# Grams in bursts of eight units, four units to a PSUM bank, in a recommendation model's interaction and MLP

## The reference

```
dots  = einsum('bfd,bgd->bfg', bottom_output, bottom_output)   # (2048, 27, 27)
pairs = dots[:, TRIL_I, TRIL_J]                                # 351 of them
x     = concatenate([bottom_mlp_output, pairs, pad], axis=1)   # (2048, 480)
for w, b in ((w0, b0), (w1, b1), (w2, b2), (w3, b3)):          # 480-1024-1024-512-256
    x = relu(x @ w.T + b)
y = x @ w_out.T + b_out                                        # (2048, 1)
```

## Time and profile before

| | |
|---|---|
| median of three runs | 501.91 us |
| profiled execution, its own time | 498.37 us |
| its span | 496.2 us |
| TensorE busy (products) | 476.7 us, 96% |
| TensorE weight loads | 440.1 us, 89% |
| VectorE, ScalarE, GpSimd busy | 199.3, 186.0, 132.1 us |
| grams on TensorE (L641) | 4096 records, 47.9 us |
| copies of grams on ScalarE (L767) | 112, 373 ns each |
| granted clock of TensorE, mean | 0.986 |

### The profile page before, as it was taken

How to read it: one execution, slowest core, us unless ns; L and a number is a source line. 1 busy time by engine, 2 the same in 40 slices (tenths; PEclk the granted TensorE clock), 3 DMA queues, 4 the chain that set the end, 5 groups by cost and what they waited for, 6 DMA issues and landing times.

```text
span 496.2 us, 17883 instructions
## 1 busy us (share of the span) xinstructions
PE 476.7 (96%) x7119; PEld 440.1 (89%) x7119; DVE 199.3 (40%) x461; ACT 186.0 (37%) x457; POOL 132.1 (27%) x242
## 2 busy tenths in 40 slices
PE   6767999999999999999999999999999999999998
PEld 5666988998989998999999998999899998999897
DVE  1155635435542453245432543255423544143211
ACT  3345633425333353325342443235332533234222
POOL 1630321121322241222222231223222141224231
PEclk9789999999999999999999999999999999999999
DMA  8996976656666566754674656755665564300000
GB/s 209 264 325 152 272 108 109 107 108 122 99 99 126 95 112 99 123 111 79 101 111 102 109 88 97 127 107 88 103 104 117 92 96 69 76 29 0 1 1 0
DMA packets 281088, 53.83 MB, mean 108 GB/s; under 512 B 265126, under 2 KB 279230, under 8 KB 281022
## 3 DMA queue, kind: packets, MB, share of 16 engines
q1 hardware_dynamic: 279090, 52.22, 55.6%
q10 hardware_dynamic: 1932, 0.61, 0.5%
HBM read 45.71 MB, written 7.09 MB: 106 GB/s over the span
## 4 chain that ended last, share of the span: by engine, by line
PE 84%; SPq 7%; DMA 6%; issue 2%; DVE 1%; ACT 1%; ACTq 0%; DVEq 0%
PE acc L690 38%; PE acc L683 23%; PE acc L685 11%; PE gram_ps L641 7%; SPq L454 5%; DMA rows<-in_r_bottom_output_dram 2%; DMA pairs<-blocks 2%; PE gram_ps L609 2%; SPq L436 1%; DMA blocks<-grams 1%; DVE xt L886 1%; PE side_ps L614 1%; PE acc L614 0%; SPq L406 0%; SPq L401 0%
## 5 line engine op out<-in xcount | busy, mean ns | idle before, releaser
L554 POOL TENSOR_TENSOR h_a<-h_full,h_a 128x256 fp32r<-128x256 f32 x96 | 71.8, 751 | 173.7 <-DVE h_a L905 173.7
L690 PE MATMUL acc<-h_a,w_hi 128*128 128x256 f32 x592 | 116.4, 288 | 0.0
L683 PE MATMUL acc<-h_a,w_hi 128*128 128x512 f32 x280 | 100.0, 401 | 0.0
L690 PEld LDWEIGHTS acc<-h_a,w_hi 128*128 128x128 f32 x592 | 94.6, 191 | 1.9 <-issue 0.2
L554 POOL TENSOR_TENSOR h_b<-h_full,h_b 128x256 fp32r<-128x256 f32 x64 | 47.1, 736 | 170.1 <-DVE h_b L905 170.1
L776 ACT ACTIVATE h_full<-acc,small_t 128x256 f32<-128x256 f32 x98 | 46.3, 474 | 121.4 <-PE acc L690 120.5
L690 PE MATMUL acc<-h_a,w_lo 128*128 128x256 f32 x296 | 79.4, 283 | 0.1
L794 ACT ACTIVATE h_full<-acc,small_t 128x256 f32<-128x256 f32 x77 | 36.5, 474 | 113.8 <-PE acc L685 113.8
L685 PE MATMUL acc<-h_a,w_lo 128*128 128x256 f32 x280 | 78.6, 281 | 0.0
L886 DVE STREAM_TRANSPOSE xt<-rows 128x512 f32<-128x512 f32 x112 | 73.5, 689 | 10.4 <-DMA rows<-in_r_bottom_output_dram 10.3
L899 DVE TENSOR_TENSOR h_full<-acc,h_full 128x256 f32<-128x256 f32 x77 | 32.7, 424 | 111.7 <-ACT h_full L794 111.7
(11 more groups left out here) (69 smaller groups left out, 555.3 us busy)
## 6 DMA issues: line engine op xcount, KB each, us to landing
rows<-in_r_bottom_output_dram SPq DMA_DIRECT2D x444, 64.0 KB, 2.1
blocks<-grams SPq DMA_DIRECT2D x30, 216.0 KB, 4.0
w_raw<-in_L_rec_w_dram SPq DMA_DIRECT2D x6, 1024.0 KB, 7.9
early_rows<-in_r_bottom_output_dram SPq DMA_DIRECT2D x12, 224.0 KB, 5.9
stage_pairs<-in_L_rec_w_dram SPq DMA_DIRECT2D x1, 1408.0 KB, 10.6
w_raw<-in_L_rec_w_dram SPq DMA_DIRECT2D x2, 512.0 KB, 7.8
mlp_rows<-r_bottom_mlp_output_dram SPq DMA_DIRECT2D x8, 128.0 KB, 2.4
pairs<-blocks SPq DMA_DIRECT2D x8, 126.0 KB
```

The lines of the kernel that those rows point to most:

```text
L554: nc.gpsimd.tensor_tensor(h[:, m, 1, :], h_full[:, slot % FULL_RING, :], h[:, m, 0, :].bitcast(F32), ALU.subtract).then_inc(split_done, 1)
L683: nc.tensor.matmul(found, weight(w_hi, layer, m, k), src.rearrange("p h n -> p (h n)"), start=(k == 0), stop=False)
L690: last = nc.tensor.matmul(found[:, 0:CHUNK], weight(wp, layer, m, k), src[:, xp, :], start=(k == 0 and n == 0), stop=(ends and n == 2))
```

## The change

The grams of a chunk are made in two bursts of eight units, at the hooks after 108 and 252 products, where there were four bursts of four. For chunks 1 to 7 four units share a PSUM bank, each in its 128 columns, so that the 16 units fill four banks. ScalarE then copies a whole bank in one instruction (`move_bank`), two of them behind each other at each burst. `grams_done` counts one a bank for these chunks, and TensorE waits for it only at the first unit of a bank. Chunk 0's own units keep their banks and copies.

```
-HOOK, FIRST_HOOK, UNITS_A_HOOK, HOOKS_A_BURST = 36, 6, 2, 2
+HOOK, FIRST_HOOK, UNITS_A_HOOK, HOOKS_A_BURST = 36, 6, 2, 4
+UNITS_A_BANK = 4
+BANKS_USED = UNITS // UNITS_A_BANK
...
+        def gram_found(d, u):
+
+            if isinstance(d, int) and d == 0:
+                return first_gram_found(u)
+            first = u % UNITS_A_BANK * P
+            return gram_ps[:, u // UNITS_A_BANK, first:first + P].rearrange("p (j f) -> p j f", f=QUAD)[:, :, 0:FEATS]
+
+        def bank_found(q):
+
+            return gram_ps[:, q, :].rearrange("p (j f) -> p j f", f=QUAD)[:, :, 0:FEATS]
+
+        def bank_place(q):
+
+            n = UNITS_A_BANK * UNIT_GROUPS
+            return grams[:, :, q * n:(q + 1) * n].rearrange("p g j -> p j g")
+
+        def banks_count(d, q):
+
+            return UNITS + (d - 1) * BANKS_USED + q + 1
...
-                sp.wait_ge(grams_done, d * UNITS + UNITS)
+                sp.wait_ge(grams_done, UNITS + d * BANKS_USED)
...
-                if isinstance(d, int) and d == 1 and u < GRAM_RING:
+                if isinstance(d, int) and d == 0:
+                    if u >= GRAM_RING:
+
+                        pe.wait_ge(grams_done, u + 1 - GRAM_RING)
+                elif isinstance(d, int) and d == 1:
                     if u == 0:
 
                         pe.wait_ge(w_done, LATE_WEIGHTS)
-                elif not (isinstance(d, int) and d == 0 and u < GRAM_RING):
-
-                    pe.wait_ge(grams_done, d * UNITS + u + 1 - GRAM_RING)
+                elif u % UNITS_A_BANK == 0:
+
+                    pe.wait_ge(grams_done, banks_count(d - 1, u // UNITS_A_BANK))
...
-            def move_gram(d, u):
-
-                act.wait_ge(gram_done, d * UNITS + u + 1)
-                if u == 0:
+            def move_bank(d, q):
+
+                act.wait_ge(gram_done, d * UNITS + (q + 1) * UNITS_A_BANK)
+                if q == 0:
 
                     act.wait_ge(spilled, d * GROUP * 16)
-                nc.scalar.activation(gram_place(u), gram_found(u), ACT.Copy).then_inc(grams_done, 1)
+                nc.scalar.activation(bank_place(q), bank_found(q), ACT.Copy).then_inc(grams_done, 1)
...
-                        move_gram(c + step[1], step[2])
+                        if step[2] % UNITS_A_BANK == UNITS_A_BANK - 1:
+                            move_bank(c + step[1], step[2] // UNITS_A_BANK)
```

More of the change, by code:

```diff
@@ L385, in samples, with first_gram_found, first_gram_place @@
             return xt[:, u % XT_RING].rearrange("p j (s f) -> p j s f", s=GROUP)[:, :, :, 0:FEATS]
-        def gram_found(u):
+        def first_gram_found(u):
             return gram_ps[:, u % GRAM_RING, 0:P].rearrange("p (j f) -> p j f", f=QUAD)[:, :, 0:FEATS]
-        def gram_place(u):
+        def first_gram_place(u):
             return grams[:, :, u * UNIT_GROUPS:(u + 1) * UNIT_GROUPS].rearrange("p g j -> p j g")
+        def gram_found(d, u):
[10 more added lines that the diff above has]
+            return UNITS + (d - 1) * BANKS_USED + q + 1
         def turned_cols(u):
@@ L640, in gram @@
                         at = slice(QUAD * s, QUAD * (s + 1))
-                        last = nc.tensor.matmul(gram_found(u)[at, j], xt[:, u % XT_RING, j, at], samples(u)[:, j, s],
+                        last = nc.tensor.matmul(gram_found(d, u)[at, j], xt[:, u % XT_RING, j, at], samples(u)[:, j, s],
                                                 start=True, stop=True, tile_position=(0, QUAD * s))
@@ L891, in early_move @@
                 dve.wait_ge(gram_done, u + 1)
-                nc.vector.tensor_copy(gram_place(u), gram_found(u)).then_inc(grams_done, 1)
+                nc.vector.tensor_copy(first_gram_place(u), first_gram_found(u)).then_inc(grams_done, 1)
             def add_halves(c, layer, m):
```

## The result

The changed kernel takes 542.7 us (median of five runs, 534.78 to 544.16) where 501.75 was the median before. The ratio is 1.0741, 95% interval 1.0704 to 1.0778. Ratio and interval rest on the three shorter of the five runs (534.78, 538.54 and 542.70 us), since the other two lie more than 1.5% above the shortest. The execution that was profiled took 543.41 us, 4.5 more than the 538.9 that the ratio gives, and the one profiled before (498.37) was 3.4 us short of its median. So the two traces differ by 45.0 us where the ratio gives 37.2.

A forecast was written before the change was run, and what follows sets the result against it. TensorE, busy all the time in chunks 1 to 6, bounds the kernel. 498.37 - 3.1 (crossings) + 31.2 (fetch) + 3.7 (chunk 0) + 11.6 (clock) = 541.8 us; with 3.5 up to the median, 545, range 520 to 564.

The forecast's parts named there:

- Fetching instructions: TensorE's bursts of eight need two instruction packets and stop for the second: 12 × 2.6 = 31.2 us in chunks 1 to 6.
- a round of 3.9 us: Time from asking for an instruction packet to using it, taken between 3.6 and 6.2 us; gives stops of 2.6 us.
- The rival that the fetch keeps up: No stops in the long bursts, only the crossings are saved: 498.8 us, faster; chance 6%.
- The rival of tiny stops: TensorE holds more instructions than counted, 14 stops of 0.24 us: 502.2 us, no change; chance 5%.
- The clock: Half of 14 stops are followed by a low TensorE clock, 1.65 us each: 11.6 us, bounds 0 and 23 or 46.
- The rival without a low clock: TensorE stops in the bursts but its clock stays up, with dense products on both sides: 533.7 us; chance 33%.
- Chunk 0: Longer bursts and two stops, less saved bursts and waits: 3.7 us lost in chunk 0, from 2.0 to 5.
- the wait near 74 us: Chunk 0: TensorE's wait for VectorE's split weights swallows the 1.47 us of the burst removed at 64 us.
- the slack at 84 us: Chunk 0: TensorE's wait for VectorE's split weights gives 1.2 us back.
- The burst: Two bursts fewer a chunk save crossings between products and grams: 0.21 + 0.30 = 0.51 us a chunk, 3.1 in six.
- ScalarE, VectorE, the queues: One bank copy of 0.6 us, bound 1.5, replaces four; transposes, spill and waits on copies cost nothing.

The follow-up runs named there:

- experiments 4: The changed kernel, bursts of eight units, with two of the four sample groups left out of each gram in chunks 1 to 7: 481.75 us, ratio 0.9634.
- 7: The changed kernel with 256 satisfied waits, which make 128 instructions, ahead of TensorE's first step: 543.23 us, ratio 1.0866.
- 2: The changed kernel with 24 products made after four units of each burst of eight, in all chunks: 505.54 us, ratio 1.0093.
- 3: The changed kernel with 12 products made after four units of each burst of eight, in all chunks: 517.94 us, ratio 1.0349.
- the pauses: Experiment 1 with satisfied waits inside the bursts at products 108 and 252, chunks 1 to 6: pauses of 5.3, 2.7, 1.6 us took 582.70, 540.59, 515.78 us.
- experiment 6: The changed kernel with bursts of four units in chunk 0 and of eight in all other chunks: 531.75 us, ratio 1.0608.
- Experiment 1: The changed kernel with bursts of four units again, keeping four units to a bank and the whole-bank copies: 499.97 us, ratio 0.9995.
- experiment 12: The changed kernel's bank layout with eight bursts of two units a chunk: 505.24 us, ratio 1.0101.
- half grams: The changed kernel with half of each gram's products left out in chunks 1 to 7: bursts of eight took 481.75 us, bursts of four 482.09.

## Why the prediction was right

**Fetching instructions** was the term that decided, and it held in mechanism and size: 12 × 2.6 = 31.2 us against 30.8 measured. The packet of a burst that stopped once started 1.3 to 2.0 us into it, where the prediction had about 1. The places held too. Ten of the twelve bursts stopped once in the middle or, in chunks 1 and 4, twice; the two whose boundary lies 37 and 15 instructions behind the start stopped less inside (1.7 and 1.3 us) and again later among products (0.4 and 1.6). Two things in it were less exact than the sum. Single stops ran from 1.3 to 2.7 us, and the two bursts that stopped twice lost 3.7 and 2.9 us where I had one stop. The 2.6 a burst was right as a mean, not as a constant. It came from a round of 3.9 us, which was chosen between 3.6 and 6.2 with an argument and not measured; that the sum came out within 0.4 us is in part luck.

The rival that the fetch keeps up is out: experiments 4 and 7 leave nothing but the number and the place of the instructions as the cause, and the stops shrink in 2 and 3 as they should. It was also what the rule of the Trainium skill, "Runtime: NRT & Kernel Launch", section "Instruction fetch mechanics", leads to, that the crossing of a block is mostly hidden. In these traces it was hidden in stretches of products, where a block lasts 15 us and more, and not in long bursts, at 1.17 us a block. The rival of tiny stops is out by the same rows.

**The clock.** 11.6 us predicted for both parts. Chunks 1 to 6 lost 9, and the stretch of 80 to 120 us of chunk 0 ran at 0.91 instead of 1.00, which is up to 3.6 us more. The guess of a half was near, and the pauses show that it is about the rate at which such stops are followed by a low clock. At the time it had no better argument than two stops out of three in the startup, so that it came out is in part luck. The rival without a low clock (533.7) is out as a mechanism, though not far off as a number: the ratio's 538.9 lies midway, and the fastest of the five runs took 534.78, with a mean clock of 0.965 where the profiled one had 0.953. The clock term varies from run to run.

**Chunk 0** was put at 3.7 us, with two low stretches at half chance 5.4. It cost 6.7 by experiment 6. The traces of the two kernels part behind the wait near 74 us: from its end to chunk 1's output row experiment 6 takes 44.95 us (74.72 to 119.67) and the changed kernel 52.15 (74.65 to 126.80), 7.2 more. In these are two stops of 2.4 and 2.3 us (2.6 each in the prediction) and four units more with one crossing less, 0.9. Experiment 6 waits 1.0 us for pairs that the changed kernel does not (1.2 in the prediction). That makes 4.6; the other 2.6 fit the two low stretches, which both came, where the forecast had one (1.65). The step that was too kind is the slack at 84 us: the wait that was to give 1.2 us back was in neither kernel.

The wait near 74 us is another matter. TensorE got there early, as I had it, and waited:

```profile
69.64 0.28 PE L716 MATMUL acc<-h_a,w_hi 128*128 128x256 f32 x1
74.65 1.12 PE L631 MATMUL side_ps<-ident,w_raw 128*128 128x128 f32 x4 [4.73 <-DVE w_lo L904]
```

The wait ended at 74.65 where the earlier trace rows had 73.64, since VectorE's queue had a transpose ahead that waited for its rows until 73.31, and the clock was low from 72.4 to 79.2. Experiment 6, without the merged bursts, has the same wait up to 74.72 and the same low clock, so this is not their doing. Experiment 1, whose chunk 0 is the same program as that of experiment 6, waited only 1.90 us there: it differs from run to run.

**The burst.** Crossings were 0.30 in the prediction and 0.31 in experiment 12. With half grams the merge gave 0.37 a chunk instead of 0.51. With full grams, no run without stops isolates it.

**ScalarE, VectorE, the queues** cost nothing, as predicted. The bank copy was mis-sized, 0.93 us instead of 0.6. It stayed inside the bound of 1.5 and cost no time that can be seen: experiment 1 is at 0.9995.

## What to carry to other kernels

Look at the rate at which an engine uses up instructions, not only at how busy it is: many tiny instructions in a row are a load on the instruction queue, and batching them makes it worse although it saves crossings. Here the queue delivered one packet of 256 instructions per 3.6 us or so. Bursts of 256 instructions stopped seldom, bursts of 384 (or the products behind them) in eight cases of twelve and bursts of 512 in all twelve. An idle time of over 2 us on TensorE was in half or more of the cases paid a second time, in a lower clock.

## What was not expected

- A low clock followed 8 of 12 pauses of 2.7 us and 12 of 12 of 5.3 us that had nothing to do with grams or fetching.
- An instruction of TensorE that only holds two satisfied waits took 0.11 us; the waits as such are not free in a burst.
- 128 such instructions ahead of the program moved chunk 1's output row by just 1.6 us (126.80 to 128.40), though they take some 14 us. That the startup, which waits for data anyway, hides the rest is how I read it, not shown.
- In the burst at product 108 of chunk 1, experiments 1, 2 and 4 stopped for 1.6, 0.9 and 1.3 us, though none of these bursts should need two packets at once. The traces show what it hangs on, though no run tried it. By the count, the boundary lies 246 or 247 instructions behind the start of this burst, so one lies also 9 or 10 ahead of it, and the packet asked for there is needed within 1.2 us. In experiment 1 it started at 131.04, behind the burst's start. In chunk 4 the boundary lies at the same place, but the packet had started at 314.61, 1.6 us ahead of the burst, and the burst ran in one piece:

```profile
130.71 1.29 PE L667 MATMUL gram_ps<-xt 128*32 128x27 f32 x123
133.38 0.25 PE L667 MATMUL gram_ps<-xt 128*32 128x27 f32 x5 [1.38 <-issue]
...
316.23 1.62 PE L667 MATMUL gram_ps<-xt 128*32 128x27 f32 x128
```

So a burst of one packet can stop as well. Why the packet started late in chunk 1 stays open.
